# Causal masks on VectorE and POOL, and an earlier start over the context, in a two-layer decoder

## The reference, cut to what matters

```
x = x + L0_attn(layernorm(x))         # causal self-attention, 16 heads of 8
x = x + L0_xattn(layernorm(x), ctx)   # attention over 6404 context rows, 16 heads of 8
x = x + L0_ffn(...); x = x + L1_attn(...)      # experts; attention across the heads of a row
x = x + L1_xattn(..., ctx); x = x + L1_ffn(...)  # 16 heads of 64 over the context; experts

scores = einsum('bhqd,bhkd->bhqk', q, k) / sqrt(8)
scores = where(tril, scores, -inf)    # in the self-attention only
out    = softmax(scores) @ v
```

## Time and profile before

| | us |
|---|---|
| median of 3 runs (lowest, highest) | 4169.25 (4164.22, 4173.83) |
| profiled execution, its time | 4169.31 |
| its span in the trace | 4167.0 |
| self-attention: first maxima tile, first values, last copy of outputs | 42.6, 69.4, 264 |
| context: first projection, first maxima tile, first scores, last copy of outputs | 287.5, 331.7, 398.0, 1464 |
| busy over the span: PE, VectorE, ScalarE, POOL | 3681.0, 2697.0, 2113.2, 2452.4 |

### The profile page before, as it was taken

One profiled execution on the slowest core, in us unless ns is written; L12 is line 12 of the kernel. 1 busy time (PEld: TensorE's weight loads), 2 busy tenths in 40 slices (PEclk: granted clock), 3 DMA queues, 4 the chain that ended last, 5 costly groups with the idle time before them and its releaser, 6 DMA issues. The chain is left out here.

```text
span 4167.0 us, 57041 instructions
## 1 busy us (share of the span) xinstructions
PE 3681.0 (88%) x21368; PEld 1516.9 (36%) x21368; DVE 2697.0 (65%) x4163; ACT 2113.2 (51%) x2503; POOL 2452.4 (59%) x1245
## 2 busy tenths in 40 slices
PE   5875888888888889868999999999999999999699
PEld 2341222222222143433444444444444444444343
DVE  4547888888888423566676666667666667674232
ACT  2442888888888923434444444444444444444221
POOL 2205656656565300424787888878888888889700
PEclk6785999999999979868999999999999999999889
DMA  2013002002000010420010100110110011011100
GB/s 72 24 38 82 1 1 33 1 1 33 1 1 1 1 44 0 181 93 13 25 29 26 30 28 27 29 28 27 28 30 28 26 29 29 25 31 31 64 12 5
DMA packets 74152, 126.07 MB, mean 30 GB/s; under 512 B 10509, under 2 KB 26459, under 8 KB 73211
## 3 DMA queue, kind: packets, MB, share of 16 engines
q1 hardware_dynamic: 73308, 121.25, 10.3%
q10 hardware_dynamic: 576, 1.18, 0.1%
HBM read 87.76 MB, written 34.64 MB: 29 GB/s over the span
## 5 line engine op out<-in xcount | busy, mean ns | idle before, releaser
L1111 POOL TENSOR_TENSOR att_total<-att_total,att_prob 128x1024 f32<-128x1024 f32 x608 | 1569.5, 2581 | 342.9 <-ACT att_prob L1337 291.5
L1337 ACT ACTIVATE att_prob<-PS 128x1024 f32<-128x1024 f32 x816 | 791.6, 1021 | 1007.5 <-PE PS L1244 1003.6
L1380 DVE TENSOR_REDUCE att_top_piece<-PS 128x1 f32<-128x512 f32 (+1 forms) x1586 | 988.7, 665 | 349.1 <-PE PS L1186 339.4
L647 DVE TENSOR_REDUCE att_top_piece<-PS 128x1 f32<-128x512 f32 (+4 forms) x1680 | 1021.0, 651 | 235.4 <-PE PS L450 140.6
L605 ACT ACTIVATE att_prob<-PS 128x1024 f32<-128x1024 f32 (+2 forms) x912 | 863.8, 1004 | 187.7 <-PE PS L489 151.6
L1257 PE MATMUL PS<-att_prob,att_vals 128*64 128x512 f32 x3264 | 792.8, 606 | 3.7 <-issue 2.5
L450 PE MATMUL PS<-cross_Kstack,cross_Qmax 49*128 49x512 bf16 (+1 forms) x1664 | 330.3, 391 | 186.7 <-DVE att_top_piece L647 166.1
L515 PE MATMUL PS<-att_prob,cross_Vst 128*32 128x512 f32 x3264 | 443.8, 606 | 0.5 <-ACT att_prob L605 0.2
L382 POOL TENSOR_TENSOR att_stage<-att_stage,att_run 128x512 f32<-128x512 f32 x160 | 203.8, 1274 | 400.0 <-ACT att_stage L586 398.7
L1186 PE MATMUL PS<-att_k_hi,att_q_hi 64*128 64x512 f32 (+1 forms) x1664 | 382.1, 458 | 64.5 <-DVE att_top_piece L1380 63.6
L450 PEld LDWEIGHTS PS<-cross_Kstack,cross_Qmax 49*128 49x128 bf16 x1664 | 92.8, 93 | 685.3 <-DVE att_top_piece L647 517.3
(11 more groups left out here) (250 smaller groups left out, 3320.3 us busy)
## 6 DMA issues: line engine op xcount, KB each, us to landing
att_vals<-values SPq DMA_DIRECT2D x192, 256.0 KB, 2.6
values<-mla_stage SPq DMA_DIRECT2D x24, 1024.0 KB, 4.2
f_w<-in_f_w SPq DMA_DIRECT2D x40, 256.0 KB, 5.3
cross_Kstack<-kparts SPq DMA_DIRECT2D x36, 204.0 KB
kparts<-att_prob SPq DMA_DIRECT2D x42, 128.0 KB, 1.8
att_vals<-values SPq DMA_DIRECT2D x16, 192.0 KB, 2.3
k_ctxT<-in_ctxT SPq DMA_DIRECT2D x1, 2448.0 KB
qparts<-att_prob SPq DMA_DIRECT2D x12, 128.0 KB, 1.8
```

Of the source, the lines that this page charges most:

```text
L647: dve.tensor_reduce(top_piece[:, n % 2, s * QT + qt, c:c + 1], PS[:, banks[item][s], 0:w], AX, ALU.max).then_inc(dve_freed, 1)
L1111: pool.tensor_tensor(so_far, so_far, prob[0:rows, j % RING, :, :], ALU.add).then_inc(summed, 1)
L1337: act.activation(prob[:, j % RING, :, :].rearrange("p a b -> p (a b)"), PSf[:, b:b + 2 * HALF], ACT.Exp, scale=scale).then_inc(exped, 1)
L1380: dve.tensor_reduce(top_piece[:, n % 2, s * QT + qt, c:c + 1], PS[:, bank_of(item, s), 0:w], AX, ALU.max).then_inc(dve_freed, 1)
```

## The change

1. Maxima of diagonal tiles (att0): VectorE reduces the columns left of the last 128 and takes the last 128 with a mask in one `tensor_tensor_reduce` (add, then max), into a column of its own. PE's by_query matmuls are gone.
2. Probabilities of diagonal tiles (att0): POOL sets the exponentials above the diagonal to zero with `affine_select`; the values' matmuls wait for it. PE's by_key matmuls are gone.
3. `clear_cross` runs on POOL in one go before the staging of att0's values.
4. SP loads Qm behind the fourth fill's stores, K's pieces 0 and 1 of att1 behind fills 7 and 11, and the rest after the last stores; ScalarE loads nothing, and does not start on tiles until all fills are split.
5. First unit of att1: the tiles with qt > 0 are copied by ScalarE, both banks at once, as bf16 into `wide_run` or one of three `wide_stage` slots; VectorE merges a slot into the running maximum and reduces it once at the end. Later units are as before.
6. `lead` in att1 is 0 for the first unit and 6 for the others; it was 10.

```diff
@@ -170,7 +174,7 @@
     def lead(n):
-        return min(12, 4 + 4 * n) if causal else 10
+        return min(12, 4 + 4 * n) if causal else (6 if n >= 1 else 0)
@@ -228,9 +232,15 @@
     def is_copied(item, s):
-        return not causal and item[0] == "m" and s == 1 and item[3] == QT - 1 and item[2] < NCH - 2
+        return (not causal and item[0] == "m" and item[1] >= 1 and s == 1 and item[3] == QT - 1 and
+                item[2] < NCH - 2)
     copied = [item for item in maxima if is_copied(item, 1)]
+    pairs = [] if causal else [item for item in maxima if item[1] == 0 and item[3] > 0]
+    pair_number = {item: i for i, item in enumerate(pairs)}
+    merge_number = {item: i for i, item in enumerate(item for item in pairs if item[2] > 0)}
+    SLOTS = 3
@@ -283,6 +296,18 @@
         return 0 if not causal or at < 0 or (par == 1 and i == 0) else at
+    masked_items = [item for item in maxima if causal and item[2] * HALF + item[4] == item[1] % HALVES * HALF +
+                    (item[3] + 1) * P]
+    masked_number = {item: i for i, item in enumerate(masked_items)}
+    reduced_up_to = [2 * len([i for i in masked_items if i[1] <= n and i[4] > P]) for n in range(UNITS)]
+    masked_up_to, count = [], 0
+    for n, kts in steps:
+        count += len([kt for kt in kts if causal and kt * P >= n % HALVES * HALF])
+        masked_up_to.append(count)
@@ -336,14 +363,27 @@
         def _(sp):
+            def wait_fill(n):
+                sp.wait_ge(out[n % OUT], 16 * PARTS * (n // OUT + 1))
...
                     sp.dma_start(dst[j, :, c:c + w], parts[:, n % OUT, j, 0:w]).then_inc(out[n % OUT], 16)
-            wait_out(sp)
-            load(sp, Qm, qparts, 0, slice(0, T), 1, qm_loaded[0])
-            for i in range(1, PIECES):
+                if n == HALVES + 1:
+                    for i in range(HALVES):
+                        wait_fill(i)
+                    load(sp, Qm, qparts, 0, slice(0, T), 1, qm_loaded[0])
+                if not causal and n >= HALVES + PIECE and (n - HALVES) % PIECE == 1:
+                    i = (n - HALVES) // PIECE - 1
+                    for k in range(HALVES + i * PIECE, HALVES + (i + 1) * PIECE):
+                        wait_fill(k)
+                    load(sp, Kst, kparts, 0, piece(i), 0, first_loaded[i])
+            for n in range(max(0, len(fills) - OUT), len(fills)):
+                wait_fill(n)
+            for i in range(max(0, (len(fills) - HALVES - 2) // PIECE), PIECES):
@@ -397,11 +439,18 @@
                 u = n // HALVES
+                for par, kt in enumerate(steps[j][1]):
+                    diagonal = kt * P - n % HALVES * HALF
+                    if causal and diagonal >= 0:
+                        lo = first_column(n, kt, par, i)
+                        pool.wait_ge(exped, number(j, par) + 1)
+                        block_ = prob[:, j % RING, par, :, lo:diagonal + P]
+                        pool.affine_select(out=block_, in_=block_, compare_op=ALU.is_ge, fill=0.0, base=lo - diagonal,
+                                           pattern=[[0, 2], [1, diagonal + P - lo]],
+                                           channel_multiplier=-1).then_inc(masked, 1)
...
                     stage_values(u + 1)
-                    if spare is not None:
-                        pool.wait_ge(staged, u + 2)
-                        spare(pool, u)
@@ -444,17 +493,11 @@
                     at = n % HALVES * HALF + qt * P
-                    diagonal = causal and c * HALF + w == at + P
...
                                       tile_position=(64 * s, 0))
-                    if diagonal:
-                        identb, by_query, _ = masks
-                        for s in range(2):
-                            i = pe.matmul(PS[:, banks[item][s], w - P:w], identb[:, :], by_query[:, :], start=False,
-                                          stop=True, skip_group_check=True)
@@ -482,19 +525,11 @@
                 lo = first_column(n, kt, par, i)
-                diagonal = kt * P - n % HALVES * HALF
-                masked = causal and diagonal >= 0
...
                                   stop=True, tile_position=(64 * s, 0))
-                if masked:
-                    identb, _, by_key = masks
-                    for s in range(2):
-                        i = pe.matmul(PS[:, 2 * (e % 2) + s, lo:diagonal + P], identb[:, :],
-                                      by_key[:, HALF - P - diagonal + lo:HALF], start=False, stop=True,
-                                      skip_group_check=True)
@@ -502,6 +537,8 @@
                 pe.wait_ge(exped, number(j, len(kts) - 1) + 1)
+                if masked_up_to[j]:
+                    pe.wait_ge(masked, masked_up_to[j])
@@ -558,10 +595,6 @@
             second(len(fills) - 1)
-            for n in range(HALVES, min(len(fills), HALVES + PIECE)):
-                act.wait_ge(out[n % OUT], 16 * PARTS * (n // OUT + 1))
-            load(act, Kst, kparts, 0, piece(0), 0, first_loaded[0])
@@ -571,12 +604,24 @@
                                        scale=-1.0).then_inc(negated, 1)
+                elif item in pair_number:
+                    c, qt, w = item[2:]
+                    act.wait_ge(max_scored, maximum_number[item] + 1)
+                    if c == 0:
+                        to = wide_run[qt - 1]
+                    else:
+                        i = merge_number[item]
+                        if i >= SLOTS:
+                            act.wait_ge(pair_merged, i - SLOTS + 1)
+                        to = wide_stage[i % SLOTS]
+                    b = banks[item][0]
+                    act.activation(to[:, :, 0:w], PS[:, b:b + 2, 0:w], ACT.Copy).then_inc(pair_copied, 1)
@@ -591,6 +636,8 @@
                 act.activation(heads_out[:, :], PS[:, PV, :], ACT.Copy).then_inc(out_copied, 1)
+            act.wait_ge(part3, len(fills))
@@ -637,23 +684,57 @@
             dve.wait_ge(cleared, 1 if clear is None else 1 + CLEARS)
+            def merge(item):
+                c, qt, w = item[2:]
+                if c == 0:
+                    return
+                i = merge_number[item]
+                dve.wait_ge(pair_copied, pair_number[item] + 1)
+                if c >= 2:
+                    dve.wait_ge(pair_merged, i - (QT - 1) + 1)
+                now = wide_run[qt - 1][:, :, 0:w]
+                dve.tensor_tensor(now, now, wide_stage[i % SLOTS][:, :, 0:w], ALU.max).then_inc(pair_merged, 1)
+                if c == NCH - 1:
+                    dve.wait_ge(pair_merged, i + 1)
+                    dve.tensor_reduce(top_piece[:, 0, :, :].rearrange("p (s t) c -> p s t c", s=2)[:, :, qt, 0],
+                                      wide_run[qt - 1], AX, ALU.max).then_inc(wide_taken, 1)
...
                     c, qt, w = item[2:]
-                    dve.wait_ge(max_scored, maximum_number[item] + 1)
+                    if item in pair_number:
+                        merge(item)
+                    else:
+                        dve.wait_ge(max_scored, maximum_number[item] + 1)
+                    diagonal = causal and c * HALF + w == n % HALVES * HALF + (qt + 1) * P
                     for s in range(2):
-                        if not is_copied(item, s):
+                        if diagonal:
+                            if w > P:
+                                dve.tensor_reduce(top_piece[:, n % 2, s * QT + qt, c:c + 1],
+                                                  PS[:, banks[item][s], 0:w - P], AX, ALU.max).then_inc(reduced, 1)
+                            if masked_number[item] >= 1:
+                                dve.wait_ge(dve_freed, freed[masked_items[masked_number[item] - 1], s][1])
+                            dve.tensor_tensor_reduce(out=masked_scores[:, s, :], in0=PS[:, banks[item][s], w - P:w],
+                                                     in1=masks[:, :], scale=1.0, scalar=MASKED, op0=ALU.add, op1=ALU.max,
+                                                     accum_out=top_piece[:, n % 2, s * QT + qt, NCH:NCH + 1]
+                                                     ).then_inc(dve_freed, 1)
+                        elif item not in pair_number and not is_copied(item, s):
...
                                               ALU.max).then_inc(dve_freed, 1)
-                    if not causal and c == NCH - 1 and qt == 0:
+                    if not causal and n >= 1 and c == NCH - 1 and qt == 0:
@@ -1737,21 +1818,17 @@
                 return pool.memset(tile[r:r + 1, :, :, at].bitcast(F32), value).then_inc(done, 1)
-            def clear_cross(pool, u):
-                if u <= 2:
-                    s = u - 1
+            def clear_cross(pool):
+                for s in range(2):
                     set_row(pool, Kcross, s, slice(0, NCTX), ONES2, cross_cleared)
-                    pool.wait_ge(cross_cleared, 2 * s + 1)
+                    pool.wait_ge(cross_cleared, 3 * s + 1)
                     set_row(pool, Kcross, s, slice(NCTX, NPAD), 0.0, cross_cleared)
```

(55 more changed lines are left out.)

13 lines of the change are left out of this document (10 added, 3 removed).

## The result

Over six runs each, the changed kernel took 4148.34 us median (4141.97 to 4154.22) and the kernel before 4171.54 (4164.22 to 4177.15): ratio 0.9947, 95% interval 0.9937 to 0.9957, so 18 to 26 us faster. Forecast were 4141, in a range of 4122 to 4160. The profiled execution after took 4141.97 us with a span of 4140.2, 26.8 under the profiled one of before; it was the fastest of the six.

A forecast was written before the change was run, and what follows sets the result against it. The prediction took PE, coupled to VectorE, to bound the self-attention loop, and VectorE's reductions the context's first maxima. Its terms, -1.3 - 12 - 6.5 - 9.2 - 8.3 + 9.2 = -28.1 us, took 4169.25 to 4141.2 us, range 4122 to 4160.

The forecast's parts named there:

- C: Context start, first projection to first context tile: early loads let PE begin sooner, -6.5 us.
- D: Maxima of the context's first unit: ScalarE copies and VectorE merges shorten them to 46.0 us, -9.2 us.
- B: Self-attention loop: masks leave PE for VectorE and POOL, -12 us, bounds -27 and +12.
- A: Self-attention start: first tile at 41.3 us through reordered Qm and K loads, -1.3 us, between -2.5 and +2.
- rival 4: Self-attention loop loses its clock, at 0.50 throughout: +33 us there, 4186 us in all; chance 0.04.
- +12 us where PE stands for it: Self-attention loop: masked maxima lengthen the half PE waits for by 0.22 us in 48 tiles, 0.1 in 16.
- The waits behind by_key: Self-attention loop: +5 us for POOL's selects, +5 us where removed masks had filled time while VectorE reduced.
- Rival 1: Self-attention's masked maximum costs 0.51 us, a pass plus a second operation: 4155 us; chance 0.15.
- 8.1 + 1 to 2 of waiting less about 2 of slack: Context start: slip in us of ScalarE's last fill copy behind the early load issues, to 322.5 us.
- Rival 2: Context start gains nothing because strips compete with stores: 4148 us; chance 0.15.
- E: Lead before the context's first scores: without ten second-unit tiles, 2.6 us for 10.9, -8.3 us.
- F: Loop over the context: the tiles removed from the lead come back there, +9.2 us.

The follow-up runs named there:

- experiment 1: Changed kernel with all context loads of Qm and K back behind the last store, piece 0 on ScalarE's queue: 4148.85 us, ratio 0.9950.
- experiment 2: Changed kernel with only Qm loaded early over the context, all of K on SP behind the last store: 4152.67 us, ratio 0.9955.
- experiment 3: Changed kernel with piece 1 of K over the context loaded behind the last store, Qm and piece 0 still early: 4148.07 us, ratio 0.9945.
- experiment 4: Changed kernel without ScalarE's copied pairs, VectorE reducing the context's first unit from PSUM as before: 4162.12 us, ratio 0.9975.
- experiment 5: Changed kernel with the context's lead back at ten tiles, also for the first unit: 4147.83 us, ratio 0.9950.
- experiment 6: Changed kernel with a context lead of 4 tiles instead of 6: 4148.19 us, ratio 0.9950.
- experiment 9: Changed kernel with the context's early loads issued by POOL instead of SP, behind the same waits: 4142.43 us, ratio 0.9927.
- experiment 10: Changed kernel with only the self-attention's part kept; context as before, with late loads, no pairs, lead of ten: 4164.18 us, ratio 0.9978.
- experiment 12: Changed kernel with POOL issuing the context's early loads, a context lead of 4, and ScalarE issuing the self-attention's Qm: 4134.73 us, ratio 0.9909.
- experiment 7: Changed kernel with the self-attention's by_query masks back on PE and plain VectorE reductions, POOL's selects kept: 4159.00 us, ratio 0.9975.
- experiment 8: Changed kernel with the self-attention's by_key masks back on PE, no POOL selects, masked maxima kept on VectorE: 4145.31 us, ratio 0.9945.

## Why the prediction was right, point by point

The sum of six steps came within 1.4 us of the trace's, which was in part luck: errors in C and D cancelled (+4.4, -2.7), and the profiled loop of B was of the short kind (below). The median is lower in gain than the profile: -23.2, not -29.5 or -26.8.

**A, right.** -1.8 for -1.3.

**B, right in the fall and in its size here, wrong in its split.** Ten profiles share this self-attention's loop, the changed kernel and experiments 1 to 6, 9, 10 and 12: the loop took 208.0 to 209.1 us in four and 212.9 to 215.7 in six, mean 212.0. By that mean B is -9.7; the profile after is of the short kind, which accounts for 4 of the 6 us between its steps' sum and the medians. The two kinds part most at the end of the loop. The last 24 us before the last copy, in the changed kernel's profile and in that of experiment 2, whose loop is 7.6 us longer:
```profile
224.84:248.84 24.00, 20.38 (x140) 6.85 (x138) 1.30 (x6) 15.37 (x22) 4.95 (x12) 0.82 0.00 1
```
```profile
232.33:256.33 24.00, 21.95 (x120) 6.40 (x116) 1.16 (x6) 12.65 (x19) 4.96 (x12) 0.61 0.00 1
```
The program is the same there, the mean granted clock is 0.82 or 0.61 of full speed, a mix of the levels 2.4 and 1.2 GHz; what decides between them wasn't found. Over the whole loop the mean is 0.69 in the four short ones, 0.65 to 0.66 in the six long ones, and 0.74 in both profiles of the kernel before. So rival 4, a loop that loses its clock, has a true core in every profile: PE's loop without the masks runs at a lower mean, and 5 to 7 us more are lost in some executions. It stays far from the 0.54 that the rival needed.

In the split, the two experiments are best set against the changed kernel's profile, since their loops have its clock (0.70 and 0.69 in the mean, 0.91 and 0.81 in the last 24 us). by_query was put at -18 + 12 = -6; experiment 7 gives 9.4 us by its loop and about 11 by the medians: 14.7 us of PE's busy time, less 5.4 of idle time. by_key was put at -16 + 5 + 5 = -6; experiment 8 gives 6.5 by its loop (18.5 busy, less 12.0 idle) and nothing in the medians, so that its size is open. The term of the sum that failed is "+12 us where PE stands for it": a half gets longer by 0.07 us and not 0.22 in 48 tiles and by nothing in 16, 3.4 us in all, and 5.4 us of waits is what experiment 7 shows. The waits behind by_key were put at 5 + 5 and came to 12, of which POOL's latency, put at 5, is next to nothing (0.5 us of PE's waits): the masks filled more time in which PE had nothing else to do than I allowed.

**The masked maximum** was put at 0.35 us between 0.29 and 0.51. It adds 0.20 to VectorE's chain, below the lower bound, since I took lengths where the next operation starts before the end. Rival 1 is out: it needed 0.51.

**C, wrong**: -2.1 for -6.5. The step that failed is the slip of the last fill's copy, "8.1 + 1 to 2 of waiting less about 2 of slack", 7 to 8 us: it slipped by 11.4. The 24 issues were counted rightly at 8.1 us, and 7.8 of them are found at fill 8's last store (experiment 2). The term that failed is the "1 to 2 of waiting": a store issued behind piece 0's strips took up to 6.8 us to land and not 1.8, so ScalarE got the buffer back 5.0 us later again. Rival 2 described the outcome, and its cause ("the strips compete with the stores") is real: it is 5.0 of the 12.8 us at fill 8's landing, and 3.1 of the 11.4 at the last copy stay even with POOL's queue. SP's place in the order is the larger part.

**D, right, its size off by 2.7 us**: the term is the strip, 3.3 us forecast and 3.0 measured, eleven times over. By the forecast's own prices it is 2 x 0.66 + 3 x 0.69 = 3.4, so the sum was a little low for them, and again the prices are lengths where the chain runs at 0.60 us an operation.

**E and F, right**: -8.3 and +8.4 for -8.3 and +9.2; unit 0 took 79.0 us for 71.6, 7.4 more for the 7.8 forecast. Together they are worth nothing that shows: experiment 5 undoes both and comes out within 1.6 us in the trace and the same in the runs.

## What to carry to other kernels

- Loads put between stores on one queue cost more than their issues: the stores behind them are issued later and land later too. Look for the engine that waits for the buffer that the delayed store frees, and give the loads to an idle engine's queue. That turned 2 us of gain at the first tile into 11 in the traces here, and the whole kernel came out 6 us faster.
- A row of the timeline that joins issues can hold a wait: over a wide window the stores of fills 8 to 11 are one row, twelve in 10.98 us, but they are nine in 4.28 us, a wait of 5.4 and three more. Read the durations and landings of the issues before giving one a price.
- Price a chain of independent operations on one engine by the distance of their starts in the timeline, not by their lengths: 0.60 against 0.68 us for reductions and merges, and for a masked maximum 0.20 against 0.28 + 0.08 us.
- Before reading a step of a few microseconds from one profile, look at how it spreads over kernels that share the code: here one loop spread by 7.6 us.

## What the runs showed of the hardware that I had not expected

- An operation with an accumulator has a second instruction of 83 ns that overlaps its successor: the pair took 0.20 us of the chain, a plain reduction of 128 columns 0.20 to 0.21.
- An issue of SP costs 0.34 us for a strip and 0.465 to 0.48 for a store, also behind twelve strips; on POOL a strip costs 0.55, on ScalarE 0.37 (4.44 us for twelve in experiment 12).
- A store of 128 KB landed 1.7 to 1.9 us behind its issue (experiment 1, 298 to 306 us); behind twelve strips on the same queue up to 6.8 us, half of a fill's landings coming only with the last strips'; beside strips on POOL's queue 2.7 to 4.4 us (experiment 9).
- The same loop ended at a mean granted clock of 0.82 in one execution and 0.61 in another, over the 24 us before its last copy, with loops 7.6 us apart.
